# Performer attention: GpSimd takes the weighing of the values, the residual addition and the scaling of later batches

## The chip, the core and the metric

The kernel runs on one core of a Trainium2 chip. Its engines are TensorE (matmuls, in the profile PE, its weight loads PEld), VectorE (DVE), ScalarE (ACT), GpSimd (POOL) and SyncE (SP, which issues the DMAs here). Each follows its own instruction list in order; they meet at semaphores only. The metric is device microseconds of one execution, lower is better: 2308.22 us for the kernel before, the median of three runs (2302.86 to 2309.53).

## The reference

The program is a chain of four transformer-like blocks over 32 batches of tokens with width 192; every block has an attention and a feed-forward part. The change lies in the first attention, a Performer (softmax kernel features) with 12 heads of 16, 64 random features, over the 87 tokens that a selection stage kept of each batch. Its core, per batch and head:

```
y = layernorm(x) * g + b                    # q = k = v = y
u = (y * d**-0.25) @ proj.T                 # 64 features
diag = 0.5 * sum((y * d**-0.25)**2)
q' = exp(u - diag - max_over_features(u)) + 1e-4
k' = exp(u - diag - max_over_tokens_and_features(u)) + 1e-4
out = q' @ (k'.T @ v) / (q' @ sum_over_tokens(k'))
x = x + out
```

Queries and keys come from the same rows, so the kernel forms only q' and brings in the difference of the two maxima through the values: each token's value row (16 values and a 1 for the denominator) is multiplied by one factor per head.

## The kernel before

`performer_stage` runs between the selection stage and a layer norm. X1 holds the residual rows `[87, 32, 192]`, Y the normalised ones, YV the scaled rows in groups of 17 per head (16 values and a one); tiles are named by stage, so `arg` is `2_performer_arg` and X1 is `l0a_x` in the profile. The 32 batches go through a software pipeline. Each engine's list is written out by hand: a loop over b calls helper functions for batch b, b - 1, b - 2 and b - 3, and the order of the calls is the order of the work.

- **GpSimd** only fills constants before the loop (L1214 to L1227) and then has nothing to do in this stage.
- **VectorE**: `prepare(c)` multiplies eight batches of Y by g (L1409), adds b (L1410) and copies them to YV (L1411). It is called before the loop for batches 0 to 7, and at b = 1, 9 and 17 for the next eight. `sum_squares(c)` (L1417, L1418) makes diag for eight batches, at b = 4, 12 and 20. In each turn: `less_top(b)` (maximum L1423, sum with diag L1426, subtraction into `arg` L1431), `find_rest(b-1)` (L1436, L1439), `find_kmax(b)` (L1443), `raise_q(b-2)` (L1448), `weigh_values(b-2)` (L1454, the factor times YV into `kv`), `find_fall(b)` (L1460), `finish(b-3)` (reciprocal L1465, product L1467, addition to X1 L1470). `take_stats` (L1476) reads rows of eight finished batches that SyncE has brought back in another layout.
- **TensorE**: `turn_tops(b)` (L1278), `features(b+1)` (L1270), `spread_tops(b)` (L1282), `turn_q(b-2)` (L1290), `contexts(b-2)` (L1298, L1301), `turn_y(b+2)` (L1260), `weigh(b-2)` (L1312). Products are in f32.
- **ScalarE**: `root(b-1)` (three passes over `arg`), `find_whole(b)`, `take_qT(b-2)`, `take_ctx(b-2)`, `take_yT(b+2)`; `square_y` (L1345), the squares of eight batches, at b = 2, 10 and 18.
- **SyncE** waits for `added`, stores each batch of X1 and reads eight of them back (L1238, L1243).

The waits that matter: `contexts(b)` waits for kv_ready before its first product (L1295); `less_top(b)` waits for ctx_done of batch b - 3 before it writes one of three `arg` tiles; `features(b)` waits for less_ready of b - 1, since the products' PSUM tile is single; `find_fall(b)` waits for `spread_tops(b)`, which stands behind `features(b+1)` on TensorE. kv, out and rden have two tiles each.

## Time and profile before

| what | value |
|---|---|
| median of three runs | 2308.22 us |
| the profiled execution | 2315.61 us |
| its span, first to last instruction | 2313.9 us |
| TensorE busy | 1693.8 us (73%), mean granted clock 0.847 |
| VectorE busy | 1288.6 us (56%) |
| ScalarE busy | 1053.5 us (46%) |
| GpSimd busy | 343.5 us (15%) |
| L1448 of the Performer loop, first and last start | 103.5 and 325.5 us |
| GpSimd busy from 103 to 350 us | 0 |

The span is the time between the first and the last instruction of the one profiled execution. A busy share is an average over many stages with different limits. The slices of the page put the Performer stage in the second to sixth fortieth of the span (57.8 us each). The granted clock is TensorE's, as a share of 2.4 GHz: 1.00 is that level, 0.50 is 1.2 GHz, and what lies between is a stretch with both.

### The profile page before, as it was taken

The page shows a single profiled execution, that of the slowest core. Times are in us where ns is not written, and L with a number is a line of the kernel's source. Part 1 is how long each engine was busy: PE and PEld are TensorE (multiplying, and loading weights), DVE is VectorE, ACT ScalarE, POOL GpSimd, SP SyncE. Part 2 cuts the span into 40 slices and gives each one's busy share as a digit, 9 for nine tenths or more (in the row PEclk, how much of TensorE's full clock was granted, in tenths as well). Part 3 has the DMA queues.
Part 4 walks back from the last instruction along what each step waited for, and adds up shares of the span by engine and source line. Part 5 has one row for each costly group of instructions (what it writes and reads, how often), then busy time and mean ns, then how long its engine had stood idle before and what let it go on. Part 6 is the DMA issues. An engine that isn't in the chain of part 4 may idle for free. (4 is left out here: it accounts for less than half of the span.)

```text
span 2313.9 us, 36221 instructions
## 1 busy us (share of the span) xinstructions
PE 1693.8 (73%) x12222; PEld 1368.8 (59%) x12238; DVE 1288.6 (56%) x2687; ACT 1053.5 (46%) x2190; POOL 343.5 (15%) x415
## 2 busy tenths in 40 slices
PE   3588879957842499966499676653893798479995
PEld 2265666846631255555499554443783698479995
DVE  6588865252157789968523559997217210643223
ACT  4466754233325578865222247883322354322221
POOL 0000000005730000001242100000000342034431
PEclk9798978979975699987699787775996699689998
DMA  4200010034540000001576200000003453457775
GB/s 85 74 10 18 19 31 13 2 98 132 167 155 1 4 7 6 4 1 26 167 226 203 78 4 8 7 3 1 13 1 120 151 184 114 134 163 222 226 212 191
DMA packets 137247, 189.85 MB, mean 82 GB/s; under 512 B 51661, under 2 KB 111213, under 8 KB 137069
## 3 DMA queue, kind: packets, MB, share of 16 engines
q1 hardware_dynamic: 116289, 146.91, 20.8%
q0 software_dynamic: 15360, 36.72, 5.4%
q10 hardware_dynamic: 5420, 3.91, 0.6%
q8 instruction: 104, 1.70, 0.3%
q14 instruction: 74, 0.61, 0.1%
HBM read 150.21 MB, written 33.68 MB: 79 GB/s over the span
## 5 line engine op out<-in xcount | busy, mean ns | idle before, releaser
L1014 DVE TENSOR_TENSOR 36_l3f_mlp_hidden<-36_l3f_mlp_gate,36_l3f_mlp_first 128x512 f32<-128x512 f32 x51 | 35.0, 687 | 173.7 <-ACT 36_l3f_mlp_gate L992 106.6
L1270 PE MATMUL 2_performer_p_u<-perf_proj,2_performer_yT 128*87 128x512 f32 (+1 forms) x204 | 96.5, 618 | 10.6 <-DVE 2_performer_arg L1431 9.4
L907 PE MATMUL 36_l3f_mlp_first<-36_l3f_mlp_xT,36_l3f_mlp_w 128*128 128x128 f32 x816 | 101.1, 278 | 0.0
L907 PEld LDWEIGHTS 36_l3f_mlp_first<-36_l3f_mlp_xT,36_l3f_mlp_w 128*128 128x128 f32 x816 | 96.9, 195 | 0.0
L1030 DVE TENSOR_SCALAR 9_l0f_mlp_y<-9_l0f_mlp_second,l0f_routing_weight 128x192 f32<-128x192 f32 x51 | 21.2, 417 | 112.2 <-DMA l0f_results<-9_l0f_mlp_y,l0f_routing_put 84.5
L992 ACT ACTIVATE 36_l3f_mlp_gate<-36_l3f_mlp_first 128x512 f32<-128x512 f32 x51 | 30.5, 597 | 115.9 <-PE 36_l3f_mlp_first L912 115.9
L1028 DVE TENSOR_TENSOR 32_l3a_mlp_y<-32_l3a_mlp_second,l3a_experts_b_rows 128x192 f32<-128x192 f32 x29 | 10.4, 358 | 130.6 <-issue 96.1
L921 PE MATMUL 36_l3f_mlp_second<-l3f_experts_w,36_l3f_mlp_hidden 128*128 x408 | 79.9, 339 | 0.0
L2643 ACT ACTIVATE l1a_p<-14_pla_f,l1a_recip 128x87 int16<-128x87 f32 x272 | 71.7, 354 | 9.2 <-DVE l1a_recip L2718 9.2
L1014 DVE TENSOR_TENSOR 22_l1f_mlp_hidden<-22_l1f_mlp_gate,22_l1f_mlp_first 128x512 f32<-128x512 f32 x29 | 19.9, 687 | 100.3 <-ACT 22_l1f_mlp_gate L992 100.3
L988 ACT ACTIVATE 32_l3a_mlp_hidden<-32_l3a_mlp_first,l3a_experts_b_cols 128x128 f32<-128x128 f32 x174 | 48.1, 375 | 60.1 <-PE 32_l3a_mlp_first L912 59.9
L1270 PEld LDWEIGHTS 2_performer_p_u<-perf_proj,2_performer_yT 128*87 128x87 f32 x204 | 33.8, 179 | 61.1 <-issue 58.5
L881 POOL DMA_INDIRECT l3f_results<-36_l3f_mlp_y,l3f_routing_put x51 | 50.2, 985 | 131.8 <-DVE 36_l3f_mlp_y L1030 131.8
L921 PEld LDWEIGHTS 36_l3f_mlp_second<-l3f_experts_w,36_l3f_mlp_hidden 128*128 128x128 f32 x408 | 64.9, 189 | 6.4 <-issue 0.3
L921 PE MATMUL 32_l3a_mlp_second<-l3a_experts_w,32_l3a_mlp_hidden 128*128 x348 | 64.3, 335 | 0.3 <-ACT 32_l3a_mlp_hidden L988 0.3
L1904 POOL PARTITION_ALL_REDUCE l1a_mx<-6_l0f_hidden_wide x1 | 0.4, 388 | 409.4 <-issue 409.4
L974 ACT ACTIVATE 36_l3f_mlp_xT<-36_l3f_mlp_turned,36_l3f_mlp_nw 128x128 f32<-128x128 f32 x102 | 31.9, 364 | 63.7 <-PE 36_l3f_mlp_turned L894 51.7
L912 PE MATMUL 36_l3f_mlp_first<-36_l3f_mlp_xT,36_l3f_mlp_w 64*128 64x128 f32 x816 | 60.2, 288 | 0.0
L907 PE MATMUL 22_l1f_mlp_first<-22_l1f_mlp_xT,22_l1f_mlp_w 128*128 128x128 f32 x464 | 58.2, 280 | 0.0
L921 PE MATMUL 9_l0f_mlp_second<-l0f_experts_w,9_l0f_mlp_hidden 128*128 x204 | 46.7, 351 | 15.7 <-DVE 9_l0f_mlp_y L1030 14.9
L921 PEld LDWEIGHTS 32_l3a_mlp_second<-l3a_experts_w,32_l3a_mlp_hidden 128*128 128x128 f32 x348 | 55.8, 190 | 4.0 <-issue 0.6
L988 ACT ACTIVATE 9_l0f_mlp_hidden<-9_l0f_mlp_first,l0f_experts_b_cols 128x128 f32<-128x128 f32 x102 | 32.1, 364 | 57.0 <-PE 9_l0f_mlp_first L912 55.6
(930 smaller groups left out, 4957.0 us busy)
## 6 DMA issues: line engine op xcount, KB each, us to landing
36_l3f_mlp_w<-in_L_ffn_w_dram SPq DMA_DIRECT2D x51, 768.0 KB
22_l1f_mlp_w<-in_L_ffn_w_dram SPq DMA_DIRECT2D x29, 768.0 KB, 4.6
32_l3a_mlp_w<-in_L_attn_W_dram SPq DMA_DIRECT2D x29, 576.0 KB, 3.9
9_l0f_mlp_w<-in_L_ffn_down_w_dram SPq DMA_DIRECT2D x51, 192.0 KB
l3a_experts_w<-in_L_attn_W_dram SPq DMA_DIRECT2D x8, 576.0 KB, 8.3
l1a_blocks<-l1a_qkb SPq DMA_DIRECT2D x192, 5.4 KB, 1.8
l1f_experts_w<-in_L_ffn_w_dram SPq DMA_DIRECT2D x8, 384.0 KB, 6.2
l2a_blocks<-l2a_qkb SPq DMA_DIRECT2D x192, 5.4 KB, 1.8
```

Source lines behind the costliest of these rows:

```text
L881: nc.gpsimd.indirect_dma_start(route.results, to(i), y[i % NY][:], None).then_inc(put[i % NY], 16)
L907: nc.tensor.matmul(to(t + a * PAIRS), of[:, t + a * PAIRS, :], at[:, 0, :], start=(t == 0), stop=True, skip_group_check=True)
L912: ins = nc.tensor.matmul(to(t + a * PAIRS), of[rows, 2 * PAIRS + t, :], at[rows, 1, :], start=False, stop=True, skip_group_check=True)
L921: ins = nc.tensor.matmul(second[j % 2][:, 0:D], hidden[j % 2][:, t, :], ex.w2[:, ds(expert[j], 1), t, :].rearrange("p a w -> p (a w)"), st ...
L974: ins = nc.scalar.activation(xT[j % 2][:, k], turned[j % 2][:, k, 0:ROWS], ACT.Identity, scale=nw[j % NW][:, k:k + 1])
L988: ins = nc.scalar.activation(out[:, t], src[:, t // PAIRS, t % PAIRS, :], func, bias=ex.b1_cols[:, ds(e, 1), t])
L992: nc.scalar.activation(out[:], src[:, 0, 0:HT, :], func).then_inc(done, 1)
L1014: v.tensor_tensor(hidden[j % 2][:], gate[j % 2][:], first[j % 2][1][:, 0, 0:HT, :], ALU.mult).then_inc(hidden_done, 1)
L1028: ins = v.tensor_tensor(y[i % NY][:], of, ex.b2_rows[:, ds(e, 1), :].rearrange("p a w -> p (a w)"), ALU.add)
L1030: ins = v.tensor_scalar(y[i % NY][:], of, route.weight[:, i:i + 1], None, ALU.mult)
L1270: ins = t.matmul(p_u[:, k, 0:(EIGHT - h) * M], yT[b % 2][:, k, :], proj[:, h:EIGHT, :].rearrange("p h m -> p (h m)"), start=True, stop=True)
L2643: ins = a(P[:, j, n, :], f[j % 2][:, n * NT:(n + 1) * NT], ACT.Copy, scale=recip[:, j, n:n + 1])
```

## The change

Three pieces of element-wise work move from VectorE to GpSimd, in the same arithmetic:

- `weigh_values(b)` (L1454) is now GpSimd's, in L1233.
- the addition of the result to X1 (L1470) is GpSimd's `add_out(b)`, L1238. VectorE's `finish` gains a wait for `added` of two batches before, since `out` has two tiles.
- `prepare` for batches 8 to 31 is GpSimd's, one batch at a time, in three instructions of 192 elements each (L1223, L1225, L1227) with a semaphore wait between them. Batches 8 to 15 come before GpSimd's loop; in the loop, turn b prepares batch b + 16. VectorE keeps batches 0 to 7 (`prepare_first`).

`square_y` moves from b % 8 = 2 to 4 on ScalarE, `sum_squares` from 4 to 6 on VectorE. Waits for prepared rows now go by y_first (batches 0 to 7) or by a count per batch.

```diff
+                def prepare(b):
+                    n = 2 * (b - PREP)
+                    g.tensor_tensor(Y[:, b, :], Y[:, b, :], gb[0:NT, 0, :], ALU.mult).then_inc(y_scaled, 1)
+                    pool.wait_ge(y_scaled, n + 1)
+                    g.tensor_tensor(Y[:, b, :], Y[:, b, :], gb[0:NT, 1, :], ALU.add).then_inc(y_scaled, 1)
+                    pool.wait_ge(y_scaled, n + 2)
+                    g.tensor_copy(YV[:, b, :, 0:DH], Y[:, b, :].rearrange("t (h e) -> t h e", h=HEADS)).then_inc(y_ready, 1)
+
+                def weigh_values(b):
+                    pool.wait_ge(q_ready, b + 1)
+                    if b >= 2:
+                        pool.wait_ge(ctx_done, b - 1)
+                    g.tensor_tensor(kv[b % 2][:, 0:HEADS, :], YV[:, b], across(arg[b % 3][:, HEADS * M:], 2, V),
+                                    ALU.mult).then_inc(kv_ready, 1)
+
+                def add_out(b):
+                    pool.wait_ge(out_ready, b + 1)
+                    g.tensor_tensor(X1[:, b, :], X1[:, b, :], out[b % 2][:].rearrange("t h e -> t (h e)"),
+                                    ALU.add).then_inc(added, 1)
...
+                pool.wait_ge(made, 12)
+                pool.wait_ge(*arrived)
+                pool.wait_ge(y_first, 1)
+                for b in range(PREP, 2 * PREP):
+                    prepare(b)
+                for b in range(NB + 3):
+                    if 0 <= b - 2 < NB:
+                        weigh_values(b - 2)
+                    if 0 <= b - 3 < NB:
+                        add_out(b - 3)
+                    if b + 2 * PREP < NB:
+                        prepare(b + 2 * PREP)
...
-                    if b % PREP == 2 and b // PREP + 1 < NB // PREP:
+                    if b % PREP == 4 and b // PREP + 1 < NB // PREP:
                         square_y(b // PREP + 1)
...
                     dve.wait_ge(rden_ready, b + 1)
+                    if b >= 2:
+                        dve.wait_ge(added, b - 1)
                     v.tensor_tensor(out[b % 2][:], o_of[:, :, 0:DH], across(rden[b % 2][:], 2, DH),
                                     ALU.mult).then_inc(out_ready, 1)
-                    dve.wait_ge(out_ready, b + 1)
-                    v.tensor_tensor(X1[:, b, :], X1[:, b, :], out[b % 2][:].rearrange("t h e -> t (h e)"),
-                                    ALU.add).then_inc(added, 1)
...
                         raise_q(b - 2)
-                        weigh_values(b - 2)
...
-                    if b % PREP == 1 and b // PREP + 1 < NB // PREP:
-                        prepare(b // PREP + 1)
-                    if b % PREP == 4 and b // PREP + 1 < NB // PREP:
+                    if b % PREP == 6 and b // PREP + 1 < NB // PREP:
                         sum_squares(b // PREP + 1)
```

VectorE's list in the turn b = 9 before, from the products of `raise_q(7)` to the next `less_top`:

```order
L1448 TENSOR_TENSOR 2_performer_arg<-2_performer_arg,2_performer_whole 87x780
L1454 TENSOR_TENSOR 2_performer_kv<-perf_yv,2_performer_arg 87x204
L1460 TENSOR_TENSOR 2_performer_arg<-2_performer_rmax,2_performer_p_top 87x12
L1465 RECIPROCAL 2_performer_rden<-2_performer_p_out 87x12
L1467 TENSOR_TENSOR 2_performer_out<-2_performer_p_out,2_performer_rden 87x192
L1470 TENSOR_TENSOR l0a_x<-l0a_x,2_performer_out 87x192
L1409 TENSOR_TENSOR perf_y<-perf_y,perf_gb 87x1536
L1410 TENSOR_TENSOR perf_y<-perf_y,perf_gb 87x1536
L1411 COPY perf_yv<-perf_y 87x96x16
L1423 TENSOR_REDUCE 2_performer_rmax<-2_performer_p_u 87x12
```

The same stretch of VectorE's list now, every turn without squares or statistics alike:

```order
L1487 TENSOR_TENSOR 2_performer_arg<-2_performer_arg,2_performer_whole 87x780
L1492 TENSOR_TENSOR 2_performer_arg<-2_performer_rmax,2_performer_p_top 87x12
L1497 RECIPROCAL 2_performer_rden<-2_performer_p_out 87x12
L1501 TENSOR_TENSOR 2_performer_out<-2_performer_p_out,2_performer_rden 87x192
L1462 TENSOR_REDUCE 2_performer_rmax<-2_performer_p_u 87x12
```

Between L1487 and L1462 the weighing, the addition and the three instructions of eight batches are gone.

GpSimd's list at the end of the constants before; the branch leaves the stage:

```order
L1223 MEMSET perf_c 128x238
L1224 MEMSET 2_performer_kv 87x51
L1225 MEMSET perf_yv 87x384
L1227 MEMSET 2_performer_kmax 87x1 x2
L1175 UNCONDITIONAL_BRANCH
```

And now, two turns of its loop in which a later batch is prepared:

```order
L1233 TENSOR_TENSOR 2_performer_kv<-perf_yv,2_performer_arg 87x204
L1238 TENSOR_TENSOR l0a_x<-l0a_x,2_performer_out 87x192
L1223 TENSOR_TENSOR perf_y<-perf_y,perf_gb 87x192
L1225 TENSOR_TENSOR perf_y<-perf_y,perf_gb 87x192
L1227 COPY perf_yv<-perf_y 87x12x16
L1233 TENSOR_TENSOR 2_performer_kv<-perf_yv,2_performer_arg 87x204
L1238 TENSOR_TENSOR l0a_x<-l0a_x,2_performer_out 87x192
```

Where GpSimd had left the stage there are five instructions a turn, and from turn 16 on the first two alone. TensorE's and SyncE's lists are as before; ScalarE's differs in the place of the squares.

## Rows read from the trace of the kernel before

**Rows 1.** Timeline, one undisturbed period: start us, us, engine, line, operation, tiles, [idle before].

```profile
141.55 0.95 DVE L1431 TENSOR_TENSOR 2_performer_arg<-2_performer_p_u,2_performer_shift 87x768 f32<-87x768 f32 x1
142.42 0.96 DVE L1436 SCALAR_TENSOR_TENSOR 2_performer_arg<-2_performer_whole,2_performer_arg 87x780 f32<-87x780 int32 x1
143.10 2.31 PE L1270 MATMUL 2_performer_p_u<-perf_proj,2_performer_yT 128*87 128x512 f32 x6
...
144.05 0.95 DVE L1448 TENSOR_TENSOR 2_performer_arg<-2_performer_arg,2_performer_whole 87x780 f32<-87x780 f32 x1
...
145.03 0.37 DVE L1454 TENSOR_TENSOR 2_performer_kv<-perf_yv,2_performer_arg 87x204 f32<-87x204 f32 x1
...
145.52 0.16 DVE L1460 TENSOR_TENSOR 2_performer_arg<-2_performer_rmax,2_performer_p_top 87x12 f32<-87x12 f32 x1
145.77 0.55 PE L1298 MATMUL 2_performer_p_ctx<-perf_yv,2_performer_few 87*128 87x204 f32 x2
...
146.25 0.35 DVE L1470 TENSOR_TENSOR l0a_x<-l0a_x,2_performer_out 87x192 f32<-87x192 f32 x1
...
147.51 0.17 DVE L1426 TENSOR_TENSOR 2_performer_shift<-2_performer_rmax,2_performer_diag 87x12 f32<-87x12 f32 x1
...
148.63 0.96 DVE L1436 SCALAR_TENSOR_TENSOR 2_performer_arg<-2_performer_whole,2_performer_arg 87x780 f32<-87x780 int32 x1
```

**Rows 2.** Timeline around the scaling of eight batches at b = 9.

```profile
154.84 0.96 DVE L1436 SCALAR_TENSOR_TENSOR 2_performer_arg<-2_performer_whole,2_performer_arg 87x780 f32<-87x780 int32 x1
158.94 1.75 DVE L1409 TENSOR_TENSOR perf_y<-perf_y,perf_gb 87x1536 f32<-87x1536 f32 x1
...
165.44 0.96 DVE L1436 SCALAR_TENSOR_TENSOR 2_performer_arg<-2_performer_whole,2_performer_arg 87x780 f32<-87x780 int32 x1
165.67 4.54 PE L1270 MATMUL 2_performer_p_u<-perf_proj,2_performer_yT 128*87 128x512 f32 x6 [0.97 <-DVE 2_performer_arg L1431]
...
173.47 0.96 DVE L1436 SCALAR_TENSOR_TENSOR 2_performer_arg<-2_performer_whole,2_performer_arg 87x780 f32<-87x780 int32 x1
```

**Rows 3.** Timeline around the sum of squares at b = 12.

```profile
179.68 0.96 DVE L1436 SCALAR_TENSOR_TENSOR 2_performer_arg<-2_performer_whole,2_performer_arg 87x780 f32<-87x780 int32 x1
...
187.74 0.96 DVE L1436 SCALAR_TENSOR_TENSOR 2_performer_arg<-2_performer_whole,2_performer_arg 87x780 f32<-87x780 int32 x1
...
196.54 0.95 DVE L1436 SCALAR_TENSOR_TENSOR 2_performer_arg<-2_performer_whole,2_performer_arg 87x780 f32<-87x780 int32 x1
```

**Rows 4.** Windows: us, PE, PEld, DVE, ACT, POOL busy, granted clock, DMA share, GB/s.

```profile
142.50:146.00 3.50, 3.50 (x25) 2.28 (x24) 3.28 (x8) 2.52 (x4) 0.00 (x0) 1.00 0.00 0
188.00:191.50 3.50, 3.50 (x5) 1.15 (x6) 2.65 (x5) 2.56 (x3) 0.00 (x0) 0.50 0.00 0
```

**Rows 5.** Timeline, `features` behind the statistics at b = 15.

```profile
210.43 2.35 PE L1270 MATMUL 2_performer_p_u<-perf_proj,2_performer_yT 128*87 128x512 f32 x6 [0.64 <-DVE 2_performer_arg L1431]
```

**Rows 6.** Timeline, VectorE around the scaling at b = 1.

```profile
95.35 1.75 DVE L1409 TENSOR_TENSOR perf_y<-perf_y,perf_gb 87x1536 f32<-87x1536 f32 x1
...
99.80 0.95 DVE L1423 TENSOR_REDUCE 2_performer_rmax<-2_performer_p_u 87x12 f32<-87x768 f32 x1
```

**Rows 7.** Groups of GpSimd by form: tiles, shapes xcount | busy us, mean ns | idle before.

```profile
L3036 POOL TENSOR_TENSOR H<-H,l1a_qb 128x1536 f32<-128x1536 f32 x1 | 3.4, 3407 | 6.9 <-issue 6.9
L3036 POOL TENSOR_TENSOR H<-H,l1a_qb 128x1152 f32<-128x1152 f32 x1 | 2.7, 2721 | 0.0
...
L1607 POOL COPY 7_l0f_router_wide<-l0f_w 96x8 f32<-96x8 f32 x1 | 0.2, 188 | 0.0
```

**Rows 8.** Timeline of another stage, where GpSimd adds beside VectorE.

```profile
1063.12 1.75 DVE L3115 TENSOR_TENSOR H<-H,l1a_qb 128x1536 f32<-128x1536 f32 x1
...
1064.87 3.41 POOL L3036 TENSOR_TENSOR H<-H,l1a_qb 128x1536 f32<-128x1536 f32 x1 [6.86 <-issue]
1064.90 3.60 DVE L3095 CAST 19_l1a_close_slot<-19_l1a_close_whole 87x768 bf16<-87x768 int16 x1
...
1069.57 0.36 DVE L3127 BATCH_NORM_STATS2 stats<-H 128x6 f32<-128x192 f32 x1
```

More of the change, by code:

```diff
@@ L1198, in performer_stage @@
             u_of = p_u[:].rearrange("t k w -> t (k w)")[:, 0:HEADS * M].rearrange("t (h m) -> t h m", h=HEADS)
-            names = ("made", "chain", "y_ready", "y_squared", "diag_ready", "proj_ready", "y_turned", "yT_ready", "u_done",
+            names = ("made", "chain", "y_first", "y_scaled", "y_ready", "y_squared", "diag_ready", "proj_ready", "y_turned", "yT_ready", "u_done",
                      "rmax_ready", "shift_ready", "less_ready", "rmax_turned", "kmax_ready", "kmax_spread", "fall_ready",
@@ L1202, in performer_stage @@
                      "q_turned", "ctx_done", "qT_ready", "ctx_ready", "out_done", "rden_ready", "out_ready", "added", "kept", "loaded", "stats_done")
-            (made, chain, y_ready, y_squared, diag_ready, proj_ready, y_turned, yT_ready, u_done, rmax_ready, shift_ready,
+            (made, chain, y_first, y_scaled, y_ready, y_squared, diag_ready, proj_ready, y_turned, yT_ready, u_done, rmax_ready, shift_ready,
              less_ready, rmax_turned, kmax_ready, kmax_spread, fall_ready, whole_ready, rest_ready, power_ready, rooted,
@@ L1209, in performer_stage, with wait_y @@
             block = ctx.enter_context(nc.Block(no_gpsimd_drain=True))
+            def wait_y(eng, b):
+                if b < PREP:
+                    eng.wait_ge(y_first, 1)
+                else:
+                    eng.wait_ge(y_ready, b - PREP + 1)
             @block.gpsimd
@@ L1255, in turn_y @@
                 def turn_y(b):
-                    pe.wait_ge(y_ready, b // PREP + 1)
+                    wait_y(pe, b)
                     if b >= 1:
@@ L1341, in square_y @@
                 def square_y(c):
-                    act.wait_ge(y_ready, c + 1)
+                    wait_y(act, (c + 1) * PREP - 1)
                     if c >= 1:
@@ L1405, in _, with prepare_first @@
                 v = nc.vector
-                def prepare(c):
-                    rows = slice(c * PREP, (c + 1) * PREP)
+                def prepare_first():
+                    rows = slice(0, PREP)
                     link(v.tensor_tensor(Y[:, rows, :], Y[:, rows, :], across(gb[0:NT, 0, :], 1, PREP), ALU.mult))
@@ L1411, in prepare @@
                     v.tensor_copy(YV[:, rows, :, 0:DH].rearrange("t b h e -> t (b h) e"),
-                                  Y[:, rows, :].rearrange("t b (h e) -> t (b h) e", h=HEADS)).then_inc(y_ready, 1)
+                                  Y[:, rows, :].rearrange("t b (h e) -> t (b h) e", h=HEADS)).then_inc(y_first, 1)
                 def sum_squares(c):
@@ L1448, in raise_q @@
                     v.tensor_tensor(arg[b % 3][:], arg[b % 3][:], whole[b % 3][:].bitcast(F32), ALU.mult).then_inc(q_ready, 1)
-                def weigh_values(b):
-                    dve.wait_ge(q_ready, b + 1)
-                    if b >= 2:
-                        dve.wait_ge(ctx_done, b - 1)
-                    v.tensor_tensor(kv[b % 2][:, 0:HEADS, :], YV[:, b], across(arg[b % 3][:, HEADS * M:], 2, V),
-                                    ALU.mult).then_inc(kv_ready, 1)
                 def find_fall(b):
@@ L1481, in _ @@
                 v.tensor_scalar(proj[:], proj[:], float(DH) ** -0.25 * LOG2E, None, ALU.mult).then_inc(proj_ready, 1)
-                prepare(0)
+                prepare_first()
                 sum_squares(0)
```

## The prediction

> **What bounds the kernel now.** I read the views in this order: the page (engine shares and the 40 slices), the timeline of one undisturbed period of the Performer loop, the timeline around its disturbed periods, the windows with the granted clock, and last the groups of GpSimd. The page says that no engine is busy for the whole 2313.9 us, so the answer must come from the stage that is touched: the Performer loop, from about 72 to 347 us of the span. Nothing outside it changes.
>
> In an undisturbed period VectorE starts its L1436 at 142.42 and again at 148.63, 6.21 us apart [rows 1]. The reader is to see two things there. VectorE has hardly a gap, but it is not alone: L1460 starts at 145.52, waiting for a transpose that stands on TensorE behind `features` (143.10, 2.31 us), and the weighed values, ready at 145.40 (145.03 + 0.37), lie until TensorE comes to them at 145.77. TensorE walks from `features` (143.10) through these products back to `features` in the same 6.21 us. So VectorE and TensorE are in balance, and a lighter VectorE alone does not shorten an undisturbed period. What costs time are the periods in which VectorE has something extra. The scaling of eight batches (L1409, 158.94) makes the L1436 distances 10.60 (154.84 to 165.44) and 8.03 us (to 173.47); the second is long because TensorE's eight-batch pause leaves its clock low and `features` then takes 4.54 us in place of 2.31 [rows 2]. The sum of squares (L1417) makes them 8.06 (179.68 to 187.74) and 8.80 us (to 196.54) [rows 3]; in 188.0 to 191.5 the granted clock is 0.50, the lower level of 1.2 GHz, against 1.00 in an undisturbed window [rows 4]. Five statistics on VectorE delay `features` as well, by an idle of 0.64 us, but without a slow `features`: 2.35 us [rows 5].
>
> **The change part by part.** *Scaling leaves VectorE.* Three calls of `prepare` go (batches 8 to 31). The first, at b = 1, pushed the next maximum from 95.35 to 99.80: 4.45 us [rows 6]. TensorE is at its lower clock there with or without it, so I take just that. The others (b = 9 and 17, alike) cost 10.60 + 8.03 - 2 x 6.21 = 6.2 us each [rows 1, 2], 12.4 together. What comes next in such a period is the ordinary balance of 6.21. Gain 16.9.
>
> *Weighing leaves VectorE.* Its 0.37 us in the middle of the period only filled the wait for L1460, so nothing is gained. But kv_ready is now on GpSimd: L1448 ends at 145.00 and TensorE wants the product at 145.77, so about 0.72 us is the whole allowance [rows 1]. `contexts` waits there, and behind it on TensorE stand `turn_y`, `weigh`, the next `turn_tops` and `features`; VectorE's next L1431 waits for ctx_done too. The trace has no such small GpSimd operation on two inputs. Its two large ones take 3407 ns for 1536 elements and 2721 for 1152; its copy of 8 elements takes 188 ns [rows 7]. Per element from the first: 2.22 ns, so 204 elements 0.45 us and nothing fixed, the low end. A straight line through both: 0.66 + 204 x 0.00179 = 1.03 us, the high end. I take 0.45 + 0.19 (the copy's fixed cost, the nearest small row) = 0.64, and 0.13 for the two semaphores, an estimate from the gap of 0.03 between L1448 and L1454 [rows 1] and as much and more for another engine. 0.77 against 0.72 costs 0.05 x 29 = 1.5 us; the ends are 0 and (1.16 - 0.72) x 29 = 12.8.
>
> The page "GPSIMD Engine Reference" of the Trainium skill (section on elementwise accounting) puts a two-input operation at about 2.6 cycles an element, and says to keep such work on VectorE. By it 204 elements are 0.44 us, and the large rows agree (2.22 ns is 2.7 cycles of 1.2 GHz); it would change the sum by nothing, but it is the rule against this change.
>
> *Adding leaves VectorE.* L1470 starts at 146.25 and frees 0.28 to 0.35 us before the next maximum. That pays only where VectorE is late: 0.28 us in each of three sums of squares and two statistics, 1.4 us. At the end of the loop the last addition, now on GpSimd, stands before SyncE's DMA: 0.64 + 0.1 in place of 0.35, a loss of 0.4.
>
> *The sum of squares moves* from b % 8 = 4 to 6, ScalarE's squaring from 2 to 4. The same instructions run once per eight batches. VectorE is late by 8.06 - 6.21 = 1.85 us before and by 1.57 after (the 0.28 above), not much less. I therefore leave the slow period after each in place (rival below).
>
> *GpSimd's queue.* Per loop turn it holds weigh, add and, for b = 0 to 15, two scalings and a copy: at my durations 0.64 + 0.61 + 0.61 + 0.61 + 0.4 = 2.9 us of 6.21, so a weigh never finds it occupied. They can meet VectorE, though. In the one place of this trace where GpSimd computes on two inputs, its first operation starts at 1064.87, just as VectorE's two-input L3115 ends (1063.12 + 1.75), and a cast of VectorE that begins 0.03 us later takes 3.60 us and ends just behind the GpSimd operation; L3127 (one input, 0.36 us) runs beside the second one undisturbed [rows 8]. So some VectorE operations stop while GpSimd reads. In my period, counted from L1431: GpSimd weighs 3.5 to 4.2, adds 4.75 to 5.4, scales 5.45 to 6.7 and copies to 7.1, while VectorE's two-input L1436 wants to start at 7.08 and the short L1426 at 5.6. I put 0.2 us on each of the 14 turns that have both loop work and scaling: 2.8 us (ends 0 and 0.7, worked out under the slow rival). The 24 operations up front, 76.6 to about 90, meet a few more: 1 us. None of this holds behind b = 15.
>
> *Sum:* 16.9 + 1.4 - 1.5 - 2.8 - 1.0 - 0.4 = 12.6 us. The profiled execution took 2315.61 us (span 2313.9), so 2303.0. That execution lies 7.4 us above the median of the three runs; taken from the median 2308.22 it is 2295.6.
>
> **The rivals.**
> 1. *The slow period behind the sums of squares goes too.* TensorE's pause there shrinks towards the 0.64 us that the statistics caused without a clock drop [rows 5]. Then each costs about 1.4 (the lateness of 1.57, a little of it caught up) in place of 4.44 (8.06 + 8.80 - 12.42) less 0.28: 2.8 x 3 = 8.3 more. 2287.3. For it: full clock for all of the stretch before. Against it: 1.57 is still most of 1.85, and squares and statistics now stand one batch apart.
> 2. *GpSimd is slow but never in VectorE's way.* 1.03 us per operation: contexts wait 0.44 us in 29 turns. 16.9 + 1.4 - 12.8 - 0.7 = 4.8 us, 2303.4. For it: the straight line through [rows 7]. Against it: the second large operation may itself have been disturbed.
> 3. *Slower: GpSimd is slow and stops VectorE.* From 1.0 us per operation on, the addition runs 4.7 to 5.8, the scalings to 7.9. L1436, due at 7.08 + 0.4, waits for the second scaling, and L1439 or L1448 behind it for the copy, so raise_q comes 0.7 later, and with it ScalarE's squarings and kv. 14 x 0.7 = 9.8; the 24 operations up front then last to about 102 us and stop L1436 and its neighbours some four times, 3.5 us. With the 12.8 and 0.7 of rival 2: 26.8 against 18.3 gained: 8.5 us slower, 2316.7. It decides from about 0.9 us per operation. For it: the 3.60 us cast in [rows 8]. Against it: in b = 16 to 31 nothing is scaled, and it needs both the long durations and the stop. The page "SBUF — State Buffer" of the Trainium skill (section "Who interferes with whom") says that a VectorE instruction with two SBUF inputs and a GpSimd one that reads SBUF exclude each other for the whole instruction. By that rule the collisions are certain and only the durations decide; the cast's row agrees with it.
>
> **How the numbers follow.** Forecast 0.48; rival 1 0.20; rival 2 0.15; rival 3 0.14; 0.03 for what I don't see. About 0.3% (6.9 us) is what a measurement tells from no change. Faster by more: nearly all of the forecast and rival 1, some of rival 2: 0.70. Slower by more: rival 3: 0.13. The rest 0.17. The range of 8 in 10 goes from 2281 (rival 1 with short GpSimd operations) to 2314 (part of rival 3); the forecast's own is 2289 to 2302.
>
> **What would show it.** In the profile after: GpSimd's L1233, L1223, L1225, L1238 near 0.6 us (right) or 1.0 (rivals 2, 3); undisturbed periods behind b = 16 at 6.2 to 6.3 us, those before at up to 6.5; TensorE's first product with YV waiting for GpSimd by under 0.1 us; no gap of 4 us on TensorE at b = 9 and 17, and 2.31 us for `features` there; `features` of 4 us still behind the sums of squares; VectorE's L1475, L1478 and L1487 at their old 0.96, 0.56 and 0.95 us, and longer where GpSimd stops them. I am wrong if undisturbed periods behind b = 16 exceed 6.4 us, or if the loop ends less than 8 us earlier.

## The result and the profile after

The changed kernel takes 2285.56 us, the median of 6 runs (2280.63 to 2287.92), against 2306.59 us for the kernel before in runs beside it (6 runs, 2299.50 to 2310.83). The ratio is 0.9899 [0.9876, 0.9923], with its 95% interval: 1.0% faster, 21.0 us by the medians, about 23 us by the ratio. The forecast had 12.6 us, or 2295.6 from the median of 2308.22. The sign was right and the median lies in the range, nearest to rival 1 (2287.3); the size was little more than half of what came.

The profiled execution after took 2280.63 us, its span is 2278.9 us. That is 35.0 us less than the profiled execution before, for which the prediction had 2303.0, and just below the range (2281). Of its page, the head and the rows of the engines:

```profile
span 2278.9 us, 36311 instructions
...
PE 1683.8 (74%) x12222; PEld 1362.8 (60%) x12238; DVE 1253.7 (55%) x2614; ACT 1053.5 (46%) x2190; POOL 416.9 (18%) x551
...
POOL 0342100007710000001242100000000332034431
```

GpSimd has 73.4 us more than the 343.5 before, VectorE 34.9 us less; GpSimd's row of slices is now busy in the second to fifth slice, where the Performer loop lies.

GpSimd's five instructions, each as the answer on its line gives it (operation, names, count, then min/median/max in ns and the first and last start in us):

```profile
L1223 POOL TENSOR_TENSOR perf_y<-perf_y,perf_gb x24: 582/588/620, 76.6 to 190.8; 87x192 f32<-87x192 f32 x24
...
L1225 POOL TENSOR_TENSOR perf_y<-perf_y,perf_gb x24: 584/586/1311, 77.3 to 191.4; 87x192 f32<-87x192 f32 x24
...
L1227 POOL COPY perf_yv<-perf_y x24: 338/341/561, 77.9 to 192.1; 87x192 f32<-87x192 f32 x24
...
L1233 POOL TENSOR_TENSOR 2_performer_kv<-perf_yv,2_performer_arg x32: 526/531/533, 100.6 to 300.0; 87x204 f32<-87x204 f32 x32
...
L1238 POOL TENSOR_TENSOR l0a_x<-l0a_x,2_performer_out x32: 585/590/1265, 113.1 to 312.3; 87x192 f32<-87x192 f32 x32
```

The medians of the four with two inputs are 0.53 to 0.59 us, near the 0.64 of the forecast and far from the 1.03 of rivals 2 and 3.

One period with scaling in it, the answer to [rows 1]: the timeline of all engines, of which the rows of VectorE, GpSimd and TensorE that matter are shown:

```profile
148.00 0.96 DVE L1475 SCALAR_TENSOR_TENSOR 2_performer_arg<-2_performer_whole,2_performer_arg 87x780 f32<-87x780 int32 x1
...
148.67 2.31 PE L1309 MATMUL 2_performer_p_u<-perf_proj,2_performer_yT 128*87 128x512 f32 x6
...
149.63 0.95 DVE L1487 TENSOR_TENSOR 2_performer_arg<-2_performer_arg,2_performer_whole 87x780 f32<-87x780 f32 x1
...
150.66 0.53 POOL L1233 TENSOR_TENSOR 2_performer_kv<-perf_yv,2_performer_arg 87x204 f32<-87x204 f32 x1 [2.79 <-DVE 2_performer_arg L1487]
...
151.10 0.16 DVE L1492 TENSOR_TENSOR 2_performer_arg<-2_performer_rmax,2_performer_p_top 87x12 f32<-87x12 f32 x1 [0.52 <-PE 2_performer_p_top L1321]
...
151.35 0.55 PE L1337 MATMUL 2_performer_p_ctx<-perf_yv,2_performer_few 87*128 87x204 f32 x2
...
151.87 0.58 POOL L1238 TENSOR_TENSOR l0a_x<-l0a_x,2_performer_out 87x192 f32<-87x192 f32 x1 [0.68 <-DVE 2_performer_out L1501]
152.42 0.59 POOL L1223 TENSOR_TENSOR perf_y<-perf_y,perf_gb 87x192 f32<-87x192 f32 x1
...
152.69 0.34 DVE L1465 TENSOR_TENSOR 2_performer_shift<-2_performer_rmax,2_performer_diag 87x12 f32<-87x12 f32 x1
...
153.09 0.58 POOL L1225 TENSOR_TENSOR perf_y<-perf_y,perf_gb 87x192 f32<-87x192 f32 x1
153.33 0.96 DVE L1470 TENSOR_TENSOR 2_performer_arg<-2_performer_p_u,2_performer_shift 87x768 f32<-87x768 f32 x1 [0.30 <-PE 2_performer_p_ctx L1340]
153.73 0.34 POOL L1227 COPY perf_yv<-perf_y 87x192 f32<-87x192 f32 x1
...
154.21 0.96 DVE L1475 SCALAR_TENSOR_TENSOR 2_performer_arg<-2_performer_whole,2_performer_arg 87x780 f32<-87x780 int32 x1
```

Three things are to be seen. The period is 6.21 us, as before. The weighing ends at 151.19 (150.66 + 0.53) and TensorE's product starts at 151.35, 1.72 us behind the start of L1487 at 149.63; before it was also 1.72 (144.05 to 145.77, [rows 1]). So kv costs nothing here. And the short L1465 takes 0.34 us in place of 0.17: it stops until GpSimd's L1223 is through, at 153.01. But L1470 behind it waits for TensorE until 153.33 anyway, with 0.30 us of idle, so the stop is swallowed.

`features` behind the first sum of squares, and one window behind the second (the columns of [rows 4]); they answer to [rows 3, 4]:

```profile
135.84 2.35 PE L1309 MATMUL 2_performer_p_u<-perf_proj,2_performer_yT 128*87 128x512 f32 x6 [0.90 <-DVE 2_performer_arg L1470]
```

```profile
187.00:190.50 3.50, 3.50 (x16) 1.96 (x17) 3.32 (x9) 2.68 (x4) 0.80 (x2) 1.00 0.00 0
```

TensorE pauses for 0.90 us and goes on at the upper level (granted clock 1.00 against 0.50 in [rows 4]); the other two (starts 186.99 and 238.52, idle 0.90 and 0.85) are alike, 2.35 us. No `features` behind any later sum is slow in this execution, where the profile before had three of three.

The end of the loop, the last statistics on VectorE, after and then before:

```profile
319.17 1.40 DVE L1507 BATCH_NORM_STATS2 stats<-l0a_x 128x6 f32<-128x192 f32 x5 [6.97 <-DMA l0a_x<-l0a_rows]
```

```profile
345.53 1.40 DVE L1476 BATCH_NORM_STATS2 stats<-l0a_x 128x6 f32<-128x192 f32 x5 [6.38 <-DMA l0a_x<-l0a_rows]
```

The stage ends 26.4 us earlier in this pair; the other 8.6 us of the 35.0 between the two spans lie behind it, in stages that the change doesn't touch. The experiments show how far this pair stands for the two kernels.

### The profile page after: what moved, and what is told of

It reads as the page before. It is cut to its first block and busy times, and to the rows that moved or that the text cites. A ratio compares the mean times of both kernels' runs of the same rounds, so it can differ in the third digit from the quotient of the medians.

```text
span 2278.9 us, 36311 instructions
## 1 busy us (share of the span) xinstructions
PE 1683.8 (74%) x12222; PEld 1362.8 (60%) x12238; DVE 1253.7 (55%) x2614; ACT 1053.5 (46%) x2190; POOL 416.9 (18%) x551
## 5 line engine op out<-in xcount | busy, mean ns | idle before, releaser
L1309 PE MATMUL 2_performer_p_u<-perf_proj,2_performer_yT 128*87 128x512 f32 (+1 forms) x204 | 84.5, 554 | 7.3 <-DVE 2_performer_arg L1470 6.2
L992 ACT ACTIVATE 36_l3f_mlp_gate<-36_l3f_mlp_first 128x512 f32<-128x512 f32 x51 | 30.5, 597 | 115.2 <-PE 36_l3f_mlp_first L912 115.2
L877 POOL DMA_INDIRECT 9_l0f_mlp_x<-l0f_rows,l0f_routing_take x51 | 49.6, 973 | 42.3 <-POOLq L106 27.0
```

The costliest lines, as they stand in the source:

```text
L877: nc.gpsimd.indirect_dma_start(x[j % NX][:], None, route.rows, take(j)).then_inc(gathered[j % NX], 16)
L992: nc.scalar.activation(out[:], src[:, 0, 0:HT, :], func).then_inc(done, 1)
L1309: ins = t.matmul(p_u[:, k, 0:(EIGHT - h) * M], yT[b % 2][:, k, :], proj[:, h:EIGHT, :].rearrange("p h m -> p (h m)"), start=True, stop=True)
```

## The experiments

Every ratio below is against the kernel before, run beside that version; a slow `features` is one that takes 3 to 4.5 us in place of 2.35.

**Which part does it, and is the slow period mine?** The theory here (A in the expectations) was rival 1: a shorter pause of TensorE keeps the clock up. Its rival (B): the squares' new place does it.

The changed kernel with squares and sums back at their old turns:

```diff
-                    if b % PREP == 4 and b // PREP + 1 < NB // PREP:
+                    if b % PREP == 2 and b // PREP + 1 < NB // PREP:
                         square_y(b // PREP + 1)
...
-                    if b % PREP == 6 and b // PREP + 1 < NB // PREP:
+                    if b % PREP == 4 and b // PREP + 1 < NB // PREP:
                         sum_squares(b // PREP + 1)
```

> The changed kernel with the squares and their sums back at their old turns (ScalarE b % 8 = 2, VectorE b % 8 = 4). Theory A (the slow period behind the sums of squares went because VectorE is late by 0.28 us less and TensorE pauses 0.90 us instead of 1.04 and a bit): nothing comes back, features stays at 2.3 us behind all three, time as the changed kernel within 2 us (about 2285). Rival B (it went because the sum stands in another place relative to the other stalls): at b = 4, 12 and 20 features of about 4 us returns, 2.5 to 3 us each, 8 us slower than the changed kernel.

2285.17 us, ratio 0.9907 [0.9873, 0.9941]: the same as the change. `features` is slow (4.05 us) behind the first sum, with the pause of 0.90 that left the clock up above, and not behind the other two. The place of the squares is worth nothing that can be measured.

The changed kernel with the addition back on VectorE:

```diff
-                    if 0 <= b - 3 < NB:
-                        add_out(b - 3)
...
-                    if b >= 2:
-                        dve.wait_ge(added, b - 1)
                     v.tensor_tensor(out[b % 2][:], o_of[:, :, 0:DH], across(rden[b % 2][:], 2, DH),
                                     ALU.mult).then_inc(out_ready, 1)
+                    dve.wait_ge(out_ready, b + 1)
+                    v.tensor_tensor(X1[:, b, :], X1[:, b, :], out[b % 2][:].rearrange("t h e -> t (h e)"),
+                                    ALU.add).then_inc(added, 1)
```

> The changed kernel with the addition to X1 back on VectorE; weighing and scaling stay on GpSimd. Theory A: VectorE's lateness at the sums of squares is 1.85 us again, TensorE's pause about 1.1, and the slow period returns behind all three: 0.28 + 2.7 us each, so 8 to 9 us slower than the changed kernel, plus 0.3 us at each of two statistics. Rival B (the place, not the length): only 0.28 x 5 = 1.4 us slower.

2293.64 us, 0.9932 [0.9907, 0.9957]; the loop (here and below, the start of its last statistics) ends at 326.62. As long as GpSimd scales, VectorE's periods without a sum or statistics alternate between 6.60 and 6.16; from b = 16 on they are 6.21. From its timeline:

```profile
131.95 0.59 POOL L1225 TENSOR_TENSOR perf_y<-perf_y,perf_gb 87x192 f32<-87x192 f32 x1
131.96 0.79 DVE L1495 TENSOR_TENSOR l0a_x<-l0a_x,2_performer_out 87x192 f32<-87x192 f32 x1
```

The addition, 0.35 us in [rows 1], takes 0.79 and ends only behind GpSimd's instruction. Here is the stop that I had priced, in a kernel where something of 0.35 us stands in its way. So the addition's move is worth more than the work that it takes from VectorE: it takes VectorE's operation on two SBUF inputs out of the place where GpSimd reads. Not all of the difference is this. The periods of this profile are 8.0 us longer in sum than those of the profile after, and 3.9 of them are two slow `features`: 4.54 us behind the second sum, and 3.15 us at 258.83, in a turn in which VectorE has no extra work. The other 4.1 are the stops and the addition itself.

The changed kernel with a needless reduction of 192 elements before each later sum, to bring TensorE's pause back to its old length:

```diff
                     dve.wait_ge(y_squared, c + 1)
+                    if c >= 1:
+                        link(v.tensor_reduce(extra[:], SQ[:, 0, :].rearrange("t (h e) -> t h e", h=HEADS), AX.X, ALU.add))
```

> The changed kernel with one more VectorE reduction of 192 elements (about 0.35 us, its result unused) in each of the three later sums of squares. Theory A: lateness 1.57 + 0.35 = 1.9 us, TensorE's pause about 1.25 us, slow features of 4 us behind all three: 9 us slower than the changed kernel. Rival B: 3 x 0.35 = 1.05 us slower and features at 2.35 us.

2289.60 us, 0.9918 [0.9893, 0.9943]. The pauses are 1.04 us as before (about 1.25 had been expected), and only the third is followed by a slow `features` (4.05).

The kernel before with only the squares moved (the edit of the change in those two lines, nothing else):

> The kernel before with only the squares and their sums moved to the new turns (4 and 6). Theory A: the lateness stays 1.85, the slow periods stay, time as the kernel before within 2 us. Rival B: the slow periods behind the sums go, 8 us faster than the kernel before.

2308.25 us, 0.9997 [0.9981, 1.0013]; slow behind one sum of three. The pauses are 1.04 us. So neither the place nor a pause of 1.04 us decides. What I had read as fixed varies.

**The parts of the move, and the costs of GpSimd that I had charged.** The kernel before with only the scaling moved to GpSimd; weighing, addition and squares stay as they were:

```diff
+                for b in range(PREP, 2 * PREP):
+                    prepare(b)
+                for b in range(NB + 3):
+                    if b + 2 * PREP < NB:
+                        prepare(b + 2 * PREP)
...
-                    if b % PREP == 1 and b // PREP + 1 < NB // PREP:
-                        prepare(b // PREP + 1)
```

> The kernel before with only the scaling of batches 8 to 31 on GpSimd; weighing, addition and the places of the squares as before. If the scaling on VectorE brought the slow periods behind the squares as well (its own pause of TensorE 4 us before them), none follows the squares at b = 12 and 20 now though VectorE is late by 1.85 us: 17 us from the scaling and up to 7 from the squares, about 2284 to 2287. If the length of the lateness decides, the slow periods stay and only the 17 us come, 2291, less what collisions of VectorE's addition with GpSimd cost (0.4 us in every second turn up to b = 15, 3 us), 2294.

2290.97 us, 0.9923 [0.9896, 0.9951]; the loop ends at 324.36. By the ratios this part brings 18 of the 23 us. Its undisturbed periods stay at 6.21, and the 3 us of collisions that were expected did not come. The reason is in GpSimd's timeline: nothing in its list waits for the loop here, so it scales all 24 batches in one go and is through at 119.2 us, before the undisturbed periods begin. Its last row:

```profile
118.87 0.34 POOL L1227 COPY perf_yv<-perf_y 87x192 f32<-87x192 f32 x1
```

While it lasts VectorE does stop: its addition takes 0.61 us in place of 0.35 at 116.13.

The opposite: the kernel before with weighing and addition on GpSimd and the squares at their new turns, the scaling of eight batches left on VectorE:

```diff
+                for b in range(NB + 3):
+                    if 0 <= b - 2 < NB:
+                        weigh_values(b - 2)
+                    if 0 <= b - 3 < NB:
+                        add_out(b - 3)
...
-                    dve.wait_ge(out_ready, b + 1)
-                    v.tensor_tensor(X1[:, b, :], X1[:, b, :], out[b % 2][:].rearrange("t h e -> t (h e)"),
-                                    ALU.add).then_inc(added, 1)
...
-                        weigh_values(b - 2)
```

> The kernel before with weighing and addition on GpSimd and the squares at the new places, the scaling of eight batches still on VectorE. The three scalings cost 4.45 + 2 x 6.2 = 16.9 us again. VectorE is late by 1.57 us at the squares, TensorE pauses 0.90. If the length decides, no slow period behind the squares: about 2306.6 - 6 = 2300. If the scaling's stalls bring them, they stay: 2305.

2303.23 us, 0.9988 [0.9975, 1.0001]: no difference that can be told. The scaling periods are there again (10.49 + 7.56 at b = 9, 12.13 + 8.03 at b = 17, where a slow `features` of 3.19 us comes first).

The changed kernel with one more GpSimd operation of 192 elements ahead of every weighing:

```diff
+                def spend():
+                    if junks[0]:
+                        pool.wait_ge(junked, junks[0])
+                    g.tensor_tensor(junk[:], Y[:, 0, :], gb[0:NT, 1, :], ALU.add).then_inc(junked, 1)
+                    junks[0] += 1
...
                     pool.wait_ge(q_ready, b + 1)
+                    spend()
```

> The changed kernel with one more two-input GpSimd operation of 192 elements (0.59 us, its result unused) between the wait for q and the weighing. The profile of the changed kernel leaves 0.1 us between the end of the weighing and TensorE's product. If the weighing is that close to the path, each of some 29 turns grows by 0.59 + 0.06 - 0.1 = 0.5 to 0.55 us: 15 us slower than the changed kernel, about 2300, and TensorE waits for GpSimd in front of the product. If TensorE has slack that I do not see, no change.

Every undisturbed period is 6.72 us, 0.51 more for 0.59 of delay, and the loop ends at 331.4, 12.2 us later than after the change. So the allowance is real and only about 0.08 us of it is left. From the answer on the line of `contexts`: its weight loads (count, min/median/max ns, first and last start), and the idle time on this line that GpSimd's weighing ended (us, times). The same answer for the changed kernel has no idle that GpSimd ended.

```profile
L1346 PEld LDWEIGHTS 2_performer_p_ctx<-perf_yv,2_performer_few x64: 186/189/338, 101.7 to 317.8; 87*128 87x128 f32 x64
...
  POOL 2_performer_kv L1242: 21.2, 55
```

The whole time was 2318.22 us (2299.33 to 2327.87), 1.004 [1.0013, 1.0067]. Some 20 us of its profile do not come from the loop: in a later stage (`l1a_context`) with the same instructions the clock is low. Its window, and then the same work in the profile after the change:

```profile
1006.00:1068.00 62.00, 58.16 (x656) 57.75 (x656) 32.95 (x65) 33.46 (x48) 0.04 (x1) 0.50 0.01 1
```

```profile
990.00:1032.40 42.40, 35.55 (x656) 34.10 (x656) 32.92 (x67) 33.03 (x48) 0.37 (x1) 0.94 0.01 2
```

656 products each, 62.0 us at a granted clock of 0.50 against 42.4 at 0.94. The run below has it too, the other sixteen profiles do not (those products take 59.0 us in these two and 38.6 to 39.2 in the rest). Both versions have operations added on GpSimd, and most of their executions are long; whether the added work brings the low clock, and how, isn't shown. What an edit does to the loop must therefore be read in the loop.

The changed kernel with five such operations in each of the turns 16 to 31, behind the addition, so that GpSimd reads beside much of VectorE's work:

```diff
                         add_out(b - 3)
+                    if 2 * PREP <= b < NB:
+                        for _ in range(5):
+                            spend()
```

> The changed kernel with five more two-input GpSimd operations of 192 elements (results unused) behind the addition in each of the turns 16 to 31, so that GpSimd reads until about 8.6 us after the start of L1470 and meets the two-input L1475. If VectorE's two-input operations stop for the whole GpSimd operation (the slow rival's mechanism), L1475 and L1478 take up to 0.6 us more in those turns and the period grows from 6.21 to 6.6 to 7.0: 6 to 12 us slower than the changed kernel. If only the first one met is delayed and the next GpSimd operation waits in its turn, 3 us. If there is no such stop, no change.

The periods from b = 16 on without a sum of squares are 6.55 to 6.83, 0.47 more in the mean; the loop ends 5.9 us later (325.07). The whole, 2313.23 us, 1.0028 [0.9997, 1.0058], again holds the slow later stage in its profile. VectorE's groups in that stretch (busy us, mean ns, idle):

```profile
L1486 DVE SCALAR_TENSOR_TENSOR 2_performer_arg<-2_performer_whole,2_performer_arg 87x780 f32<-87x780 int32 x16 | 18.6, 1164 | 0.0
...
L1481 DVE TENSOR_TENSOR 2_performer_arg<-2_performer_p_u,2_performer_shift 87x768 f32<-87x768 f32 x15 | 14.3, 954 | 9.8 <-PE 2_performer_p_ctx L1351 9.8
L1473 DVE TENSOR_REDUCE 2_performer_rmax<-2_performer_p_u 87x12 f32<-87x768 f32 x14 | 13.2, 943 | 0.0
L1489 DVE TENSOR_SCALAR 2_performer_whole<-2_performer_whole 87x780 int32<-87x780 int32 x16 | 12.9, 805 | 0.6
...
L1476 DVE TENSOR_TENSOR 2_performer_shift<-2_performer_rmax,2_performer_diag 87x12 f32<-87x12 f32 x14 | 4.9, 354 | 0.5
```

Three that read SBUF alone grow, from 957, 562 and 168 ns (the medians of these operations after the change) to 1164, 805 and 354; the two that read the product in PSUM, L1481 and L1473, do not (954 and 943 after the change as well), though GpSimd computes beside them. Together that is 0.64 us a turn, of which 0.47 reach the period.

**What else stands in the loop.** At b = 4 TensorE goes four times over its list of products in `features`, which makes the one period of 11.40 us (11.97 in the run with the scaling alone). The changed kernel without that:

```diff
-                    again = 4 if b == 4 else 1
+                    again = 1
```

> The changed kernel without the repeated products of features at b = 4 (three of four repetitions, which only keep TensorE busy, are left out; the result is the same). In the changed kernel's profile that turn lasts 11.40 us and features already runs at 2.31 us one turn earlier. If the clock no longer needs them, the turn is 6.2 us: 5.2 us faster than the changed kernel, about 2280. If the clock falls without them, features takes 4 us in the first turns: no gain, or up to 5 us of loss.

2279.62 us, 0.9893 [0.9870, 0.9915]: that period is 6.26, and the loop ends at 315.44. The clock came up without it: it is 1.00 in 103.0 to 109.0. In this profile `features` is slow behind the first sum (4.05), and also at 247.36, in a turn in which VectorE has nothing extra and TensorE had no long pause:

```profile
247.36 3.12 PE L1309 MATMUL 2_performer_p_u<-perf_proj,2_performer_yT 128*87 128x512 f32 x6
```

That is one turn behind the statistics that follow a sum, and so are the 3.15 us at 258.83 and the 3.19 us (at 215.35) of the two versions above.

The changed kernel with the two lumps that are left cut into small pieces: the sum of squares by batch and the statistics by tile, two to a turn (`small` does one batch's sum or one tile's statistics), with the factor of the sum taken into ScalarE's squares:

```diff
+                    small(b, 0)
                     if b < NB:
                         find_fall(b)
...
-                    if b % PREP == 6 and b // PREP + 1 < NB // PREP:
-                        sum_squares(b // PREP + 1)
+                    small(b, 1)
```

> The changed kernel with VectorE's sums of squares cut into single batches (0.35 us each, two a turn in turns 5, 6, 7 and 8 of eight, the factor taken into ScalarE's square) and the statistics cut into single tiles (two a turn in turns 1 to 4 of eight), in the slots that the weighing and the addition left. The stalls of the changed kernel (1.5 + 1.9 + 1.9 us over the periods around b = 6, 14, 22) go if the slots hold 0.35 us: 5 us faster than the changed kernel, about 2280. If the slots are smaller, the eight turns grow by up to 0.3 us each and most of it comes back.

2281.63 us, 0.9899 [0.9877, 0.9920]; the loop ends at 314.36. From its timeline, one piece in front of `find_fall` and one in front of the maximum:

```profile
137.08 0.33 DVE L1462 TENSOR_REDUCE 2_performer_diag<-perf_sq 87x12 f32<-87x192 f32 x1
137.68 0.16 DVE L1512 TENSOR_TENSOR 2_performer_arg<-2_performer_rmax,2_performer_p_top 87x12 f32<-87x12 f32 x1 [0.26 <-PE 2_performer_p_top L1323]
...
138.29 0.34 DVE L1462 TENSOR_REDUCE 2_performer_diag<-perf_sq 87x12 f32<-87x192 f32 x1
138.55 0.94 DVE L1482 TENSOR_REDUCE 2_performer_rmax<-2_performer_p_u 87x12 f32<-87x768 f32 x1
...
139.91 0.95 DVE L1490 TENSOR_TENSOR 2_performer_arg<-2_performer_p_u,2_performer_shift 87x768 f32<-87x768 f32 x1 [0.21 <-PE 2_performer_p_ctx L1342]
```

Each piece fills a wait that was there: two of 0.3 us a turn fit, 0.26 and 0.21 us of idle are left, and behind b = 4 all periods but the last are 6.20 to 6.21.

Both together:

> Both of the last two: 10 us faster than the changed kernel if both hold, about 2275.

2272.22 us (2269.14 to 2282.48), 0.9862 [0.9838, 0.9886]: the fastest version here. The loop ends at 309.14.

The kernel before once more, for a second profile:

> The kernel before once more, for a second profile. If the slow period behind a sum of squares follows from VectorE's lateness of 1.85 us and the scaling's stalls, it stands behind all three sums again. If it comes by chance, some are missing, and the loop is shorter by about 2.7 us for each.

2301.82 us, 0.9996 [0.9980, 1.0013]. From its timeline, TensorE behind the sum at b = 12, where [rows 3] have the period of 8.80:

```profile
187.63 2.35 PE L1270 MATMUL 2_performer_p_u<-perf_proj,2_performer_yT 128*87 128x512 f32 x6 [1.04 <-DVE 2_performer_arg L1431]
```

The pause is 1.04 us, as in the first profile of this kernel, and `features` takes 2.35 there, not 4.54. None of the three sums has a slow period behind it, and the loop ends at 337.65, not 345.53.

**How much of a profile is chance.** Two more profiles of each of the two kernels, unchanged.

> The kernel before once more, profile only. By chance: slow periods behind zero to three of the sums of squares, 8 in 18 so far over all kernels with a TensorE pause of 1.04 us there.

> The changed kernel once more, profile only. If the shorter pause (0.85 to 0.90 us) makes slow periods rarer: none or one of three (3 in 15 so far over all kernels with that pause). The undisturbed periods stay at 6.21 us and the loop ends within 2 us of 319.

> The kernel before, profile only, as e13. If slow periods belong to the kernel before, at least one of its three later profiles has two or more; if they are rare everywhere, none has.

> The changed kernel, profile only, as e14: none or one slow period if the shorter pause makes them rarer, undisturbed periods of 6.21 us.

2306.39 and 2307.67 us before, 2282.55 and 2287.11 after. The kernel before shows slow `features` behind 3, 0, 2 and 0 of its three later sums; the changed one behind 0, 1 and 1. The third profile before has one behind the first statistics too, 4.00 us behind a pause of 0.65 with a granted clock of 0.54 in 206.4 to 209.9, where [rows 5] have 2.35 us behind 0.64. So a pause of that length is not safe either. The slow one of the second profile after, with the same idle of 0.90 as its fast fellows:

```profile
187.50 3.82 PE L1309 MATMUL 2_performer_p_u<-perf_proj,2_performer_yT 128*87 128x512 f32 x6 [0.90 <-DVE 2_performer_arg L1470]
```

Now the loop can be summed up over four profiles of before and three of after. Each term is read from VectorE's starts of L1436 (L1475 after), as time above 6.205 us a period where it is a disturbance:

| term | before, four profiles | after, three | mean gain | forecast |
|---|---|---|---|---|
| start of the first (b = 0), us | 90.9, 91.5, 91.5, 90.9 | 91.8, 90.6, 91.3 | 0.0 | -1.0 (24 operations up front) |
| first two periods (scaling at b = 1), whole | 18.4, 19.5, 16.4, 18.0 | 12.3, 14.0, 14.4 | 4.5 | 4.45 |
| two periods at b = 9, excess | 6.2, 5.5, 6.1, 5.9 | 0.0 | 5.9 | 6.2 |
| two periods at b = 17, excess | 6.3, 5.6, 6.8, 5.8 | 0.0 | 6.1 | 6.2 |
| squares and statistics, excess | 14.2, 7.3, 11.6, 7.3 | 5.3, 6.8, 6.5 | 3.9 | 1.4 |
| kv on GpSimd; stops in 14 turns | none | none | 0.0 | -1.5; -2.8 |
| last period to the last statistics | 30.6, 29.2, 29.2, 28.9 | 30.8, 30.7, 30.5 | -1.1 | -0.4 |
| end of the loop, us | 345.5, 337.7, 340.6, 335.7 | 319.2, 321.0, 321.7 | 19.3 | 12.6 |

## Why the prediction was right in sign and short in size

Two steps of it failed. The collisions of VectorE with GpSimd in the loop were charged with 2.8 us (and kv with 1.5, the 24 operations up front with 1.0), where the loop shows none: the stopped instruction stands in front of a wait. And the slow period behind each sum of squares was left in place on both sides as if it belonged to the program, where the same kernel has it in some executions only. With them a smaller term was mis-sized, the addition at the statistics. Point by point:

1. *The bound: lumps on VectorE, not its load.* Right. Undisturbed periods stay at 6.21 us although VectorE has 0.72 us less work in each; its waits for TensorE grow instead (0.52 and 0.30 us in the period above). With weighing and addition moved, and the squares, but not the scaling, nothing can be told from no change (0.9988); with the scaling moved alone 18 of the 23 us are gained (0.9923).

2. *The three scalings.* Right, 16.5 us against 16.9, though that it fits so well is in part luck. In [rows 2] the second period's slow `features` went into the price as fixed; its size varies (the two periods' excess is 5.5 to 6.8), but all four profiles have it. The first two periods vary more, from 16.4 to 19.5 us before and from 12.3 to 14.4 after, with the turn in which the clock comes up; the pair of profiles at the top gives 6.1 us there, the means 4.5 for the 4.45 of the forecast.

3. *kv on GpSimd.* The allowance was right to within its reading: 0.59 us more made each period 0.51 longer. The charge of 1.5 us was wrong. The operation takes 0.53 us, not 0.64, and TensorE comes 1.72 us behind L1487's start, as before. The steps that failed are the 0.19 taken from the small copy and the 0.13 for semaphores, together 0.77 against 0.72: in the period above L1233 starts 0.08 us behind L1487's end (150.58 to 150.66), and its end is 0.16 us ahead of the product. The weight load for that product starts earlier, at 151.28, which fits the 0.08 us that the delayed weighing found to be left.

4. *Collisions in the loop, 2.8 us.* This is the largest term that failed, with its mechanism right and its place wrong. The sign on record for it, periods of up to 6.5 us before b = 16, did not come: they are 6.21. VectorE does stop beside GpSimd's operations, L1465 for about 0.17 us in ten of these 14 turns. But with the addition and scalings at 151.9 to 153.7, the one VectorE instruction on SBUF in that stretch is the short L1465, and behind it stands a wait of 0.30 us for TensorE that swallows the 0.17. I had counted from L1431 and L1436 and looked for what starts late, and not asked whether the stopped one stood in front of a wait. The addition put back into this stretch (6.60 and 6.16 in turn; with the sums and statistics some 4 us in the loop) and the five extra operations (0.47 a turn) show what it costs elsewhere. The page "SBUF — State Buffer" of the Trainium skill (section "Who interferes with whom") has these pairs exclude each other for the whole instruction; the 0.79 us of the addition beside L1225 agrees.

5. *The 24 operations up front, 1.0 us.* They meet VectorE as said:

```profile
83.85 0.55 DVE L1465 TENSOR_TENSOR 2_performer_shift<-2_performer_rmax,2_performer_diag 87x12 f32<-87x12 f32 x1
...
92.78 0.84 DVE L1478 TENSOR_SCALAR 2_performer_whole<-2_performer_whole 87x780 int32<-87x780 int32 x1
```

0.55 in place of 0.17 and 0.84 in place of 0.56. Two such stops are 0.66 us; the start of the first period moves by -0.9 in the first pair and by 0.0 in the means. The charge of 1.0 us is in no mean. GpSimd stops as well: one L1225 takes 1.31 us in place of 0.59, which nobody waits for.

6. *The addition and the sum of squares, 1.4 us.* Of the 3.9 measured, 1.9 comes without any slow `features`: squares and statistics cost 7.3 us before and 5.3 after where nothing slow stands behind them. Each sum gives 0.22 (1.69 to 1.47), near the 0.28 counted, each of the two statistics about 0.6 (1.04 to 0.45 for the first), twice what was counted. The rest, 2.0 us in the mean, is slow periods: behind five sums and one statistics in four profiles before, behind two sums in three after. I left the slow period in place on both sides, which was the second step that failed: its presence in three of three periods of one profile was taken as a property of the kernel, and rival 1 as its removal. It is neither. The same kernel has it behind 3, 0, 2 and 0 of three sums.

7. *The tail.* -1.1 us in the means for -0.4. The last addition on GpSimd is 0.59 us for 0.35; the first pair has 0.59 us more of the wait for the DMA (6.97 for 6.38). The distance varies by 1.7 us among the profiles before, so more can't be said.

Points 3, 4 and 5 are 5.3 us charged and about 0 found, points 6 and 7 add 1.8: with 0.35 less for the scalings that is the way from 12.6 to 19.3. The whole time shows 23 us by the ratio. The mean spans of these seven profiles differ by 24.2 us, 4.9 of them behind the loop; there the profiles of one kernel differ by up to 9 us among themselves (before, 1961.4 to 1970.3; after, 1959.7 to 1963.7), so whether anything of the change reaches behind the loop stays open.

Of the rivals, 2 and 3 fall with the 0.53 to 0.59 us of the operations. Rival 1 had the nearest number and the wrong reason in part. How far it holds stays open: over all kernels here a slow `features` stands behind 9 of 24 later sums where the pause is 1.04 us (7 of 18, not 8, when the expectation above was written), and behind 5 of 21 where it is 0.85 to 0.90. A shorter pause may make it rarer; such counts don't show it. A slow one behind a pause of 0.65 us, and three one turn behind the statistics without a long pause, speak against the length of one pause as the whole cause. What decides it from one execution to the next isn't seen in any view.

The page "GPSIMD Engine Reference" of the Trainium skill (section on elementwise accounting) was the rule against this change. Its price per element agrees with the large rows; at 192 elements the measured 0.588 us is 3.06 ns an element, above the 2.22 of the large one in [rows 7]. Its advice is to keep such work on VectorE. That does not hold here: GpSimd takes 1.52 us for the scaling of a batch (0.59 + 0.59 + 0.34), VectorE took 0.56 (an eighth of 1.75 + 1.75 + 0.96), and the kernel is 1.0% faster, since nobody waits for it.

## What to carry to other kernels

Where two engines are in balance, a slower idle engine is worth having for lumps of work that stall the pair, not for the small pieces that fill a wait; and a lump that can be cut into pieces of a wait's size may stay where it is (the sums by batch, 0.33 us in a wait of 0.5). When you price a stop of one engine by another, find the stopped instruction and ask whether it stands in front of a wait. And take a dip of the clock from several profiles before it goes into a sum: in one profile it looks like part of the program.

## What the runs showed of the hardware

- GpSimd on 87 partitions in f32: two inputs of 192 elements 0.588 us, the product of 204 elements with a factor per group of 17 in 0.531, a copy of 192 in 0.341. Behind a semaphore of VectorE it starts 0.08 us later.
- Beside GpSimd's operations on two inputs three of VectorE's instructions on SBUF stop (957 to 1164 ns, 168 to 354), a TENSOR_SCALAR on a single input too (L1489, 562 to 805 ns), though not the statistics of [rows 8]; the two that read PSUM do not (954 and 943 ns).
- After one and the same pause (1.04 us with the same instructions in front) the granted clock in 188.0 to 191.5 us was 0.50 in one execution and 1.00 in another. One later stage takes 42.4 us at 0.94 or, in two versions with added work, 62.0 us at 0.50, which is nearly as much as this change brings.
